# A two-layer block with mLSTM: values centred once in the retention, the last batch's finish moved into the router stage

## The reference

```python
x = x + L0_xattn(layernorm(x), ctx, ctx)     # retention, 4 heads of 128
x = x + L0_ffn(layernorm(x))                 # ternary weights
x = x + L1_xattn(layernorm(x), ctx, ctx)     # mLSTM, 16 heads of 32
x = x + L1_ffn(layernorm(x))                 # 32 experts, top 4, and a shared one

# mLSTM, for one batch and head, with q from x and k = v = ctx
D = exp(log_D - max_log_D)                   # from gates of q and k, lower triangle
C = (q @ k.T / sqrt(dh)) * D
normalizer = maximum(abs(C.sum(-1)), exp(-max_log_D))
h = (C / (normalizer + EPS)) @ v             # dh = 32
hn = (h - mean(h)) * rsqrt(var(h) + EPS)     # over the 32 of a head
out = hn * ln_scale
```

## Time and profile before

| | |
|---|---|
| time, median of 3 runs | 1312.12 us (1309.41 to 1313.61) |
| profiled execution, its own time | 1313.15 us |
| its span in the profile | 1311.4 us |
| TensorE busy | 1100.4 us, 84% |
| VectorE busy | 844.2 us, 64% |
| ScalarE busy | 519.1 us, 40% |
| GpSimd busy | 431.1 us, 33% |
| mean granted TensorE clock | 0.929 of full |

### The profile page before, as it was taken

One profiled execution on the slowest core, in us unless ns is written; L12 is line 12 of the kernel. 1 busy time (PEld: TensorE's weight loads), 2 busy tenths in 40 slices (PEclk: granted clock), 3 DMA queues, 4 the chain that ended last, 5 costly groups with the idle time before them and its releaser, 6 DMA issues. The chain is left out here.

```text
span 1311.4 us, 22130 instructions
## 1 busy us (share of the span) xinstructions
PE 1100.4 (84%) x6197; PEld 826.9 (63%) x6198; DVE 844.2 (64%) x1585; ACT 519.1 (40%) x1089; POOL 431.1 (33%) x336
## 2 busy tenths in 40 slices
PE   6999799788896859999529996799999999999842
PEld 6989666434443439888528773677777777777630
DVE  2436359778875438999637794667677676766415
ACT  2332152466663258777214242233333333333310
POOL 0010001111100201877742001266566566655420
PEclk8999899999997879999759998899999999999975
DMA  7331500100000675662064312679789889778539
GB/s 258 107 108 66 209 0 0 17 1 0 0 1 32 230 229 160 196 224 96 0 222 182 57 60 71 187 176 232 184 237 237 191 237 232 187 188 187 86 59 374
DMA packets 116541, 181.01 MB, mean 138 GB/s; under 512 B 13609, under 2 KB 48681, under 8 KB 116496
## 3 DMA queue, kind: packets, MB, share of 16 engines
q1 hardware_dynamic: 96112, 137.14, 32.0%
q0 software_dynamic: 18080, 38.85, 15.2%
q10 hardware_dynamic: 2304, 4.46, 0.9%
HBM read 138.50 MB, written 46.67 MB: 141 GB/s over the span
## 5 line engine op out<-in xcount | busy, mean ns | idle before, releaser
L2168 POOL DMA_INDIRECT y_d<-x_eo,x_ox x80 | 169.6, 2120 | 138.3 <-ACT x_eo L2321 111.6
L1516 POOL DMA_INDIRECT x_g<-r_d,x_ix x82 | 87.4, 1066 | 150.0 <-issue 117.9
L2225 PE MATMUL x_h<-x_w_hi,x_t_hi 128*128 x320 | 127.7, 399 | 2.2 <-DVE x_t_lo L2337 2.2
L2226 PE MATMUL x_h<-x_w_lo,x_t_hi 128*128 x320 | 127.5, 398 | 0.0
L2227 PE MATMUL x_h<-x_w_hi,x_t_lo 128*128 x320 | 127.3, 398 | 0.0
L209 POOL TENSOR_TENSOR ln_rstd<-ln_ve,powers 128x2 f32<-128x2 f32 (+1 forms) x40 | 26.3, 657 | 263.0 <-DVE ln_ve L203 263.0
L2337 DVE TENSOR_TENSOR x_w_lo<-w,x_w_hi (+1 forms) x64 | 109.5, 1751 | 0.1
L2297 ACT ACTIVATE x_gs<-x_h 128x256 f32<-128x256 f32 x80 | 30.7, 384 | 192.6 <-PE x_h L2227 177.4
L2337 DVE TENSOR_TENSOR x_t_lo<-x_xb,x_t_hi 128x512 fp32r<-128x512 f32 x80 | 55.2, 691 | 43.8 <-ACT x_t_hi L2292 43.8
L2244 PE MATMUL x_o<-x_w_hi,x_avt_hi 128*128 x160 | 73.0, 456 | 1.4 <-issue 0.7
L1233 ACT ACTIVATE h_d<-h_negm,h_g 128x256 f32<-128x256 f32 x128 | 63.7, 497 | 25.0 <-DVE h_negm L1408 22.1
(11 more groups left out here) (350 smaller groups left out, 2725.9 us busy)
## 6 DMA issues: line engine op xcount, KB each, us to landing
w<-in_L_ffn_w SPq DMA_DIRECT2D x32, 1024.0 KB, 7.9
h_negm<-negm_d SPq DMA_DIRECT2D x16, 1024.0 KB, 8.6
w<-in_L_ffn_w SPq DMA_DIRECT2D x32, 512.0 KB, 9.9
raw<-in_L_ffn_w SPq DMA_DIRECT2D x3, 2816.0 KB, 16.5
x_res<-in_x SPq DMA_DIRECT2D x8, 512.0 KB, 5.9
ctx_in<-in_ctx SPq DMA_DIRECT2D x8, 512.0 KB, 4.9
kt_d<-ct SPq DMA_DIRECT2D x8, 512.0 KB, 4.5
m_kt<-kt_d SPq DMA_DIRECT2D x8, 512.0 KB, 3.7
```

Of the source, the lines that this page charges most:

```text
L1516: nc.gpsimd.indirect_dma_start(out=xg[q][s][:], out_offset=None, in_=r_d, in_offset=bass.IndirectOffsetOnAxis(ap=ix[q][:, s:s + 1], axis=0 ...
L2168: nc.gpsimd.indirect_dma_start(out=y_d[s], out_offset=bass.IndirectOffsetOnAxis(ap=ox[q][:, s:s + 1], axis=0), in_=eo[q][s][:], in_offset= ...
L2225: nc.tensor.matmul(hbank[s][:], hi[:, k, :], w13p[0][:, at, k, :], start=k == 0, stop=False)
L2226: nc.tensor.matmul(hbank[s][:], hi[:, k, :], w13p[1][:, at, k, :], start=False, stop=False)
```

## The change

Five things, in one edit:

1. In the retention, after a batch's values are multiplied, VectorE subtracts from the context in `cx[u]` its mean over each head's 32 columns (`centre`: reduce, scale, subtract), and SP stores the result to DRAM as `vc_d` (`keep_values`) before it loads the context of two batches later into the slot. The mLSTM loads its values from `vc_d`. `mean` on VectorE and `centre` on GpSimd are gone from the mLSTM; `square` waits for the division alone and stands after group 1 instead of 2, `variance` after group 2 instead of 3.
2. The last batch is no longer divided and finished in `mlstm`. Its raw result, in a buffer `tail` that lives on, is finished in the router: VectorE divides at b = 0, sums squares at b = 1 and adds at b = 4, ScalarE squares after `turned(0)`, GpSimd multiplies by ln_scale at the end of b = 1 and takes the power in two halves of 16 columns at the end of b = 2 and 3.
3. Finer loads: separate semaphores for queries and keys, for values, and for the two halves of the broadcast rows; a DMA of the rows now brings 8 heads in pieces of 256 numbers. The loads of batch 0 stand after the gate rows of batch 5, those of batch 1 after the rows of batch 0.
4. One weighing per group: one instruction over 4 heads (1536 columns) and one count, so the next scores wait for the whole of it.
5. In the router VectorE begins with `moments(0)`; the wait for the gate weights and their copy stand after `mean_square(0)`. Some buffers share memory with `tail`, `rt_lost` and `rt_prod`.

```diff
@@ retention, sync
+            def keep_values(b, u):
+                sp.wait_ge(vc_ready, b + 1)
+                sp.dma_start(vc_d[ds(b, 1)].rearrange("b p n -> p (b n)"),
+                             cx[:, u].rearrange("p c d -> p (c d)")).then_inc(vc_out[u], 16)
...
-                    sp.wait_ge(ct_ps, 4 * i + 2 * u + 2)
+                    keep_keys(2 * i + u)
+                    keep_values(2 * i + u, u)
+                    sp.wait_ge(vc_out[u], 16 * i + 16)
                     sp.dma_start(cx[:, u], ctx_rows[:, ds(at_b, CB), :]).then_inc(c_in[u], 16)
-                    keep_keys(2 * i + u)
@@ retention, vector, called at the end of batch()
+            def centre(u):
+                heads = cx[:, u].rearrange("p c (h e) -> p c h e", e=DH)
+                steps.then(nc.vector.tensor_reduce(vmean[:], heads, AX.X, ALU.add))
+                steps.then(nc.vector.tensor_scalar(vmean[:], vmean[:], 1.0 / DH, None, ALU.mult))
+                nc.vector.tensor_tensor(heads, heads, vmean[:].unsqueeze(3).to_broadcast([P, CB, NH, DH]),
+                                        ALU.subtract).then_inc(vc_ready, 1)
@@ mlstm, sync
         def decays(b, u):
-            for half in range(2):
-                sp.dma_start(nm[:, u, :, half, :],
-                             negm_d[ds(b * NH, NH), half * P:(half + 1) * P]
...
+            for f in range(2):
+                sp.dma_start(nm[:, u, HF * f:HF * (f + 1), 0:2, :].rearrange("p h c s -> p h (c s)"),
+                             negm_d[ds(b * NH + HF * f, HF), :]
...
-            if b in (2, 3):
-                values(b - 2, b - 2)
-                sp.wait_ge(q_stored[b - 2], 16)
-                scores(b - 2, b - 2)
+            if b == 5:
+                values(0, 0)
+                sp.wait_ge(q_stored[0], 16)
+                scores(0, 0)
...
-        for u in range(2):
-            decays(u, u)
+        decays(0, 0)
+        values(1, 1)
+        scores(1, 1)
+        decays(1, 1)
@@ mlstm, gpsimd
-        with steps.loop(0, B // 2, 6) as i:
+        with steps.loop(0, B // 2 - 1, 6) as i:
             for u in range(2):
-                centre(2 * i + u, u)
                 finish(2 * i + u, u)
+        finish(B - 2, 0)
@@ mlstm, scalar
-                if k == 2 and not first:
+                if k == 1 and not first:
                     square(b - 1, 1 - u)
@@ mlstm, tensor: scores()
-                if j % HH == 0:
-                    after(pe, c_ready, 2 * n - 1 + j // HH)
+            after(pe, c_ready, n)
...
@@ mlstm, vector
-            for f in range(2):
-                heads = slice(HH * f, HH * (f + 1))
-                dve.wait_ge(qk_ps, 2 * n + f + 1)
-                nc.vector.scalar_tensor_tensor(cm[:, k % 2, heads], qk[:, heads, 0:3 * P], float(DH) ** -0.5,
...
+            dve.wait_ge(qk_ps, n + 1)
+            nc.vector.scalar_tensor_tensor(cm[:, k % 2], qk[:, :, 0:3 * P], float(DH) ** -0.5,
...
-                if k == 1 and not first:
-                    mean(b - 1, 1 - u)
-                if k == 3 and not first:
+                if k == 2 and not first:
                     variance(b - 1)
...
-        divide(B - 1, 1)
-        mean(B - 1, 1)
-        variance(B - 1)
+        nc.vector.tensor_copy(tail.floor, floor_t[:, :, (B - 1) * NH:B * NH])
@@ experts, router, gpsimd
             for b in range(B):
                 mean_square(b)
                 if b + 2 < B:
                     norm.power(pool, powers, b + 3, CB)
+                if b == 1:
+                    tail_scale()
+                if b in (2, 3):
+                    tail_power(b - 2)
@@ experts, router, vector
-            dve.wait_ge(gwt_ps, 1)
-            nc.vector.tensor_copy(gwt[:], lbank[:, 0:KD * NE].rearrange("p (k n) -> p k n", n=NE)).then_inc(gwt_sb, 1)
...
             mean_square(0)
+            dve.wait_ge(gwt_ps, 1)
+            nc.vector.tensor_copy(gwt[:], lbank[:, 0:KD * NE].rearrange("p (k n) -> p k n", n=NE)).then_inc(gwt_sb, 1)
...
+                if b == 0:
+                    tail_divide()
+                if b == 1:
+                    tail_variance()
+                if b == 4:
+                    tail_add()
```

More of the change, by code:

```diff
@@ L999, in _, with __init__, take, mlstm @@
         residual(NT - 1, 1)
-def mlstm(nc, st, sem, sbuf, psum, scratch_dram, a, x, ctx_rows, ident, powers, early, kt_d, upto):
+class Tail:
+    W = DH + 1
+    def __init__(self, st, sbuf):
+        n = CB * NH
+        self.all = sbuf(st, "tail", [P, 4096])
+        at = [0]
+        def take(size):
+            at[0] += size
+            return self.all[:, at[0] - size:at[0]]
+        heads = lambda v: v.rearrange("p (c h e) -> p c h e", c=CB, h=NH)
+        columns = lambda v: v.rearrange("p (c h) -> p c h", c=CB)
+        self.raw, self.h, self.sq = heads(take(n * self.W)), heads(take(n * DH)), heads(take(n * DH))
+        self.nrm, self.var, self.rs, self.floor = (columns(take(n)) for _ in range(4))
+def mlstm(nc, st, sem, sbuf, psum, scratch_dram, a, x, ident, powers, early, tail, kt_d, vc_d, upto):
     BH = B * NH
@@ L1481, in _, with experts @@
         mask(0, 1, 0)
-        batches(lambda lo, hi: steps.loop(lo, hi, 12), lambda *v: batch(*v, first=True), batch,
+        batches(lambda lo, hi: steps.loop(lo, hi, 10), lambda *v: batch(*v, first=True), batch,
                 lambda *v: batch(*v, final=True))
-        divide(B - 1, 1)
-        mean(B - 1, 1)
-        variance(B - 1)
-def experts(nc, st, sem, sbuf, psum, scratch_dram, y_d, a, x, ident, powers, out):
+        nc.vector.tensor_copy(tail.floor, floor_t[:, :, (B - 1) * NH:B * NH])
+def experts(nc, st, sem, sbuf, psum, scratch_dram, y_d, a, x, ident, powers, lns, tail, out):
     r_d = scratch_dram("r_d", [T, D + NE + 1])
```

185 lines of the change are left out of this document (106 added, 79 removed).

## The result

The changed kernel takes 1297.83 us (median of 4 runs, 1296.97 to 1301.78) against 1311.70 for the kernel before, run beside it: 13.9 us less; the ratio of the means is 0.9901 with a 95% interval of 0.988 to 0.9922.

What follows compares the result with a forecast made beforehand. The prediction saw VectorE bounding the mLSTM batch loop, with TensorE close behind. Its terms 0 - 8 + 15 - 18 + 5 = -6 gave 1307 from 1313.15, set at 1306.0 us for the median, range 1283 to 1317.

Steps and rivals of the forecast that it cites:

- Retention, 0: Retention: centring adds 2.6 us per batch to VectorE but fits its idle time, cost 0; 2 if cover were gone.
- Front, -8: Start of the mLSTM: moved loads and smaller pieces bring the first mask at 475 instead of 483.2, -8 us.
- Batch loop, +15: mLSTM batch loop: batches take 22.0 us instead of 19.08, 2.9 more each, +15 us in all.
- the collision: mLSTM loop: GpSimd's product and sum hold VectorE's mask and division in every batch, making it 22.0 us instead of 18.1.
- rival (b): mLSTM loop: TensorE gaps lower the granted clock; if fall and collision persist, 16 us more, 1322 us; chance 0.15.
- Last batch and tail, -18: End of the mLSTM stage: 28 us instead of 45.9 from the last batch's first weighing, -18 us.
- Router, +5: Router: GpSimd's added pieces delay the rows of batches 2 to 4 by 2.5, 5.4 and 8.3 us, +5 us.
- TensorE's 2.8 us of slack: Router: batch 2's rows are ready at 692.9, TensorE turns them at 695.75; this slack was subtracted from 8.3 us.
- (a): mLSTM loop: the collision hardly occurs, batches take 18.1 us, total -30, 1282 us; chance 0.24.
- The rule by which the power blocks as well: mLSTM loop: GpSimd's power also blocks VectorE, 3.5 us more in six batches, 1328 us; chance 0.03.

Runs made afterwards that it cites:

- the late variance with halves: Changed kernel with variance behind the next batch's fourth weighing (except in the last batch) and each group weighed in two halves: 1273.14 us, ratio 0.9716.
- the late variance: Changed kernel with the variance behind the fourth weighing of the next batch again, except in the last batch: 1274.42 us, ratio 0.9736.
- the run with TensorE kept busy: Changed kernel with each batch's first group of weighted values computed twice on TensorE: 1296.77 us, ratio 0.9907.

## Why the prediction was right or wrong

**Retention, 0: right.** The trace moved by 0.1 us, and leaving the centring out gained nothing that could be seen.

**Front, -8: right**, -7.7 from stretch to stretch. Its parts came out near as well: the store 6.65 us earlier (6.5), 3.3 lost behind the added loads (4), 4.2 from the smaller pieces (3 to 4). But as forecast these parts add up to -6, not to the -8 that I put into the sum, so the last 2 us of the hit are luck.

**Batch loop, +15: right in sign and mechanism, wrong in size; it measured +8.8.** The step that failed is "VectorE's own work falls to about 15.4 us, below TensorE's 17.7. That alone gives 18.1 us per batch". The 17.7 was read from the earlier trace rows as TensorE's own pace, 4.43 us per group. But those scores were matmuls that followed VectorE's weighing half by half: 1.72 us from 564.96 to 566.68, of which TensorE needs 0.89. Its own work is 15.0 us per batch, and the loop without the collision runs at 16.8, with VectorE busy 96% of it and not TensorE setting the pace. That a row of matmuls holds such waits is shown twice: the late variance with halves has TensorE busy 16.3 us per batch instead of 15.3 without a longer batch, the kernel before with one weighing 16.4 instead of 17.7. The first two batches, which have little or nothing to finish, came together 1.9 us shorter than before, where my sum had them 1 longer. They don't show the floor alone, since TensorE's clock also left its 0.50 sooner there, 7.4 us after the first weighing instead of 10.1. With the collision I laid out 22.0 and the five later batches measured 21.2, which is +10.7 over the kernel before instead of +13.9. So the collision was priced too low (3.9 over the floor, measured 4.4, clock included) on a floor 1.3 too high, and the two errors cancelled in part.

**The clock** was my rival (b), with the condition that it persist. It did, in every batch from the second, and the loop was still faster than laid out. I had let the persistent fall add 16 us to the 22.0; the run with TensorE kept busy shows 0.8 us per batch of it, 1.3 by its batches without a fall. What I had written for the mean, that a later end makes the next batch miss the collision, may be the reason the price is small. The trace fits it in part: the batches in which the power ended 1.2 us after the first weighing took 23.0 and 22.3 us, those in which it ended up to 0.9 us before it 19.3 to 20.8. But none missed the collision altogether, and no run tests this.

**Last batch and tail, -18: -21.3.** The step that was off is "the variance of batch 6 ends 17 to 18 us into the last batch"; it ended at 14.3. The chain behind it was right, 10.2 us (forecast 10.1). I had carried over the 18.1 of my loop batch, where the measured ones had it at 14.8 to 16.7.

**Router, +5: +6.0**, right, by two errors that cancel: the start gained 2.7 instead of 0.3, and the pieces on GpSimd cost 8.7 instead of 5.3. Both come largely of one mistake: I let TensorE's 2.8 us of slack absorb part of the delay, but TensorE, begun without the wait for the gate weights, had used that slack up. The rows of batches 2, 3 and 4 came 2.5, 5.3 and 8.1 us later, forecast 2.5, 5.4, 8.3.

**The rivals.** (a), a loop that hardly collides, did not happen: from the third batch on product or sum held a mask or a division in every one. The floor that its price was built on, 18.1, was wrong too: the late variance, a kernel whose division is not held, is at 1274, below the 1282 that I gave. The rule by which the power blocks as well is refuted by a mask of 1.21 us inside a power.

What stays open is how the 4.4 us divide in a single batch. Keeping the clock up changed where the collision fell, so 0.8 for the clock and 3.6 for the hold are the difference of two loops, not of one cause taken out of the same schedule.

## What to carry to other kernels

Before an engine's busy time is used as a floor, look whether its instructions follow another engine's pieces: here 4.43 us a group were 0.7 more than the 3.74 without the waits, which a busy share does not show. When a step on GpSimd is moved earlier or later by one slot, lay it beside VectorE's two-input instructions again; here one group was worth 21.6 us of a 1300 us kernel, more than the 13.9 that the whole change had brought, while the part on GpSimd that blocks nothing (the power) is the one to lay over the division. And work pushed into the next stage should go into an engine's known idle time ahead of a wait (6.7 us here), not in small pieces in front of instructions that others wait for.

## What the runs showed of the hardware that I had not expected

- Inside the changed kernel's loop a gap of 4.2 us on TensorE stood beside about 7 us at a granted clock of 0.50, one of 4.1 beside 10, one of 2.7 beside 3.4. With the late variance the gap before the third group's scores was 1.31 us and the clock stayed at 1.00 over five batches. With the values computed twice, gaps of 1.59, 1.75 and 1.76 us left it at 1.00, and gaps of 1.75, 1.74 and 1.52 stood beside a fall of about 3 us each: the length of the gap alone does not decide.
- Computing the same weighted values twice in the gap kept the clock at 0.97 on the loop's mean and cost nothing that could be measured: a ratio of 0.9907 against 0.9901.
- GpSimd is held as well as VectorE: its product with ln_scale for two halves took 3.22 to 3.49 us in the changed kernel's batches and 2.50 in the router, with VectorE's masks beside it in the loop.
- Scores of four heads issued together took 0.89 us, the same scores in two halves that each wait for VectorE 1.72, and the profile counts both as busy throughout.
